# A two-layer graph kernel: the turn of the exponentials as a product with scaled diagonals, the mask put in by TensorE, the node products spread over the second pass

## The chip, the cores and the metric

The kernel runs on one core of a Trainium2 chip. The metric is the device time of one execution in microseconds (us). TensorE is called PE in the rows, VectorE DVE, ScalarE ACT, GpSimd POOL and SyncE SP.

## The reference

```python
h = relu(layernorm(x))                                  # x: 64 graphs x 128 nodes x 128 channels
# layer 0
D = abs(h[:, :, None, :] - h[:, None, :, :])            # every pair of nodes of a graph
s = leaky(batchnorm(D @ W1.T + b1), 0.01) @ W2.T + b2   # one score per pair; statistics over all pairs
A = softmax(where(adj > 0, s, -9e15), axis=-1)
y = leaky(batchnorm((A @ h) @ Wg.T + bg), 0.01)
x = x + concat([h, y]) @ Wt.T + bt
# layer 1: graph attention on relu(layernorm(x)) with W and a, softmax over the other axis, elu; x = x + that
```

All in float32, with 64 graphs.

## The kernel before

The 64 graphs are handled in couples of two and in 16 quads of four. Scores are symmetric, so a pair of nodes is computed once, by its distance d = 1 to 64. Eight distances of a couple make a chunk of 2 x 1024 columns: 8 chunks per couple, 16 per quad, 256 in all.

The first pass forms the products of W1 with the absolute differences of all chunks, for the statistics, and stores six of each eight chunks' products in DRAM (kept_products). The second pass goes over the chunks again, from the statistics on. A kept chunk is loaded by SP into a ring of ten buffers. The other two of each eight (numbers 2 and 7, "plain") are made again: VectorE subtracts (again, L294, both inputs in SBUF) and takes the absolute value (L1107), TensorE multiplies (L767). A plain chunk has one of two buffers, so again waits on prod2_ready until the products of the chunk before the last have read it. ScalarE applies batch norm and leaky ReLU to every chunk (L654), and TensorE multiplies by W2 (scores, L877) for each two chunks.

Around it each quad j has steps at fixed chunk numbers, written in one line: EVAC 24, DIST_T 25, TURN 27, SUM 41, SCORES 43, EXP 45, NORM 48, TURN_P 49, COPY 51, MIX 53, Y 56, Y_SUMS 57, each plus 16 j. Every engine runs the loop over n in its own queue and does its part of a step when it comes to it. In order:

- take_rows and turn_dist (L899) and take_turned (L1188) bring the scores to one row per node; POOL stores them askew to DRAM (L483), and loads them back (L489) so that row i holds its own distances; sum_half (L496) adds the part that wraps around. All this stands in POOL's one queue.
- att_sum (L906, L907) on TensorE forms s_half plus its transpose in att[0], a PSUM bank (4).
- att_scores on VectorE adds NEG times no_edge (L1204), takes the row maximum (L1207) and subtracts it (L1208). exps (L666) on ScalarE writes prob.
- att_norm on VectorE sums (L1213), takes the reciprocal (L1214) and multiplies prob with it (L1215).
- att_turn (L914) on TensorE transposes prob into att[1] (bank 5), att_copy (L1220) copies it to SBUF, att_mix (L921) multiplies it with h_nat, y_to_nodes (L662) and y_sums (L1224) finish.

h_nat holds at that time h times Wg: weighted_nodes (L852, eight passes for a quad) on TensorE and nodes_out (L632) on ScalarE make it. Quads 0 and 1 come before the second pass, and quads 2 to 15 in the first 21 chunks of it, two in each three chunks (mix_at), in banks 4 and 5 in turn. mask_l1 (L507) makes the mask of the second layer on POOL, in iterations 5 to 12. After the 256 chunks 59 more steps finish the last quads. Then comes the second layer.

Of the kernel before, what the change touches and what calls it, by code (L numbers as in the profile page):

```python
# [86 lines left out]
def two_layers(nc, x, adj, adj_t, w1_tt, wg_t, wt1_t, wt2_t, l1_w, l1_wt, cols, bt_rows,  # L87
# [8 lines left out]
    with ExitStack() as ctx:  # L96
# [51 lines left out]
        def late(at, n):  # L148
            return early[:, at:at + n]

        def by_graph(t):
# [6 lines left out]
        prob = by_graph(late(2048, 512))  # L158
# [17 lines left out]
        soft = sb("soft", [128, 4, 3, QUAD])  # L176

# [35 lines left out]
        s_sum, s_masked, dve_att, s_shifted, exp_done, prob_ready, prob_turned, prob_tr_ready, out_mm, y_ready = (  # L213
            sem(n) for n in ("s_sum", "s_masked", "dve_att", "s_shifted", "exp_done", "prob_ready", "prob_turned",
                             "prob_tr_ready", "out_mm", "y_ready"))
        x_out, x_folded = sem("x_out"), sem("x_folded")
# [81 lines left out]
        EVAC, DIST_T, TURN, SUM, SCORES, EXP, NORM, TURN_P, COPY, MIX, Y, Y_SUMS = 24, 25, 27, 41, 43, 45, 48, 49, 51, 53, 56, 57  # L298
# [58 lines left out]
        def _(sp):  # L357
# [35 lines left out]
            def load_half(j):  # L393
                sp.wait_ge(late_stored[j - BY_POOL], 16)
                sp.wait_ge(s_sum, j)
# [28 lines left out]
        def _(pool):  # L424
# [73 lines left out]

# [9 lines left out]

            for j in range(NQ):
                if j < BY_POOL:  # L510
                    store_skew(j)
                    load_half(j)
                sum_half(j)
                if 5 <= j < 5 + MRING:
                    mask_l1(j - 5)
            pool.wait_ge(bn2_var, 1)
# [8 lines left out]
        def _(act):  # L525
# [138 lines left out]
            def exps(j):  # L664
                act.wait_ge(s_shifted, j + 1)
                nc.scalar.activation(prob[:, :, :], s_shift[:, :, :], ACT.Exp).then_inc(exp_done, 1)  # L666

            for n in range(CHUNKS + TAIL):
# [10 lines left out]
                if mix_at(n) is not None:  # L679
                    nodes_out(mix_at(n))  # L680
# [53 lines left out]
        def _(pe):  # L734
# [146 lines left out]
            def at_zero(n):  # L881

                pe.wait_ge(weighted_ready, NQ)
# [4 lines left out]
            def at_one(n):  # L888

                pe.wait_ge(weighted_ready, NQ)  # L890
# [11 lines left out]
            def att_sum(j):  # L902
                pe.wait_ge(half_summed, j + 1)
                at_zero(QCH * j + SUM)
# [452 lines left out]
```

## Time and profile before

| | |
|---|---|
| median of 3 runs | 1147.15 us (1144.66 to 1148.58) |
| profiled execution | 1145.85 us, span of its instructions 1143.7 us |
| second pass | from 668 to about 1005 us, its last quads to 1037 us |
| busy, share of span | PE 92%, DVE 91%, ACT 88%, POOL 49% |
| mean granted TensorE clock | 0.987 of full |

The span is the time from the first to the last instruction. The remaining 2.15 us of the profiled execution lie around it. Busy shares are means over stages with different limits.

### The profile page before, as it was taken

The page shows a single profiled execution, that of the slowest core. Times are in us where ns is not written, and L with a number is a line of the kernel's source. Part 1 is how long each engine was busy: PE and PEld are TensorE (multiplying, and loading weights), DVE is VectorE, ACT ScalarE, POOL GpSimd, SP SyncE. Part 2 cuts the span into 40 slices and gives each one's busy share as a digit, 9 for nine tenths or more (in the row PEclk, how much of TensorE's full clock was granted, in tenths as well). Part 3 has the DMA queues.
Part 4 walks back from the last instruction along what each step waited for, and adds up shares of the span by engine and source line. Part 5 has one row for each costly group of instructions (what it writes and reads, how often), then busy time and mean ns, then how long its engine had stood idle before and what let it go on. Part 6 is the DMA issues. An engine that isn't in the chain of part 4 may idle for free.

```text
span 1143.7 us, 17677 instructions
## 1 busy us (share of the span) xinstructions
PE 1055.3 (92%) x6486; PEld 473.0 (41%) x6486; DVE 1037.4 (91%) x1382; ACT 1002.7 (88%) x1268; POOL 558.6 (49%) x314
## 2 busy tenths in 40 slices
PE   3999999999999999999999989999999999965997
PEld 1333333333333433333333444233333333355997
DVE  5999999999999999999999975999999999845887
ACT  4888999999999999999999969999999999814987
POOL 6586668777767867767777700111122213101420
PEclk9999999999999999999999989999999999987999
DMA  6443444444444444444444497999999999650012
GB/s 180 165 158 156 166 168 173 176 157 183 177 169 185 170 175 157 184 179 173 164 166 194 179 354 247 354 350 318 351 331 335 344 328 347 238 155 1 29 48 74
DMA packets 99059, 233.30 MB, mean 204 GB/s; under 512 B 9120, under 2 KB 46464, under 8 KB 98976
## 3 DMA queue, kind: packets, MB, share of 16 engines
q1 hardware_dynamic: 86704, 219.97, 52.4%
q0 software_dynamic: 2240, 7.34, 1.7%
q10 hardware_dynamic: 10032, 4.89, 1.6%
q8 instruction: 52, 0.85, 0.3%
q14 instruction: 31, 0.25, 0.1%
HBM read 124.43 MB, written 107.74 MB: 203 GB/s over the span
## 4 chain that ended last, share of the span: by engine, by line
PE 50%; DVE 27%; ACT 15%; issue 7%; ACTq 1%; POOL 0%; DMA 0%; DVEq 0%
PE psum L767 17%; DVE store L294 11%; PE psum L777 9%; ACT store L654 7%; PE psum L781 7%; DVE plain_st L1075 5%; PE psum L877 4%; ACT store L573 3%; PE psum L757 1%; PE psum L985 1%; DVE store L1107 1%; PE psum L967 1%; PE psum L950 1%; PE psum L968 1%; DVE ln_st L1012 1%
## 5 line engine op out<-in xcount | busy, mean ns | idle before, releaser
L294 POOL TENSOR_TENSOR store<-h_ext 128x2048 f32<-128x2048 f32 (+1 forms) x96 | 386.7, 4030 | 119.8 <-PE psum L767 115.9
L767 PE MATMUL psum<-store,w1tt_sb 128*64 128x512 f32 x1792 | 421.4, 598 | 19.4 <-ACT store L573 19.1
L294 DVE TENSOR_TENSOR store<-psum,h_ext 128x2048 f32<-128x2048 f32 x160 | 363.7, 2273 | 1.3 <-ACT h_ext L543 1.3
L573 ACT ACTIVATE store<-store 128x2048 f32<-128x2048 f32 x160 | 305.0, 1929 | 11.3 <-DVE store L294 8.1
L654 ACT ACTIVATE store<-store,st 128x1024 f32<-128x1024 f32 x192 | 227.9, 1240 | 0.0
L767 PEld LDWEIGHTS psum<-store,w1tt_sb 128*64 128x64 f32 x1792 | 122.2, 136 | 254.6 <-issue 224.8
L777 PE MATMUL psum<-store,w_twice 128*64 128x512 f32 x768 | 201.1, 601 | 7.0 <-DVE early L1040 3.5
L294 DVE TENSOR_TENSOR store<-h_ext 128x2048 f32<-128x2048 f32 x64 | 146.3, 2286 | 17.2 <-PE psum L767 17.2
L1075 DVE BATCH_NORM_STATS2 plain_st<-store 128x6 f32<-128x512 f32 x256 | 160.4, 676 | 0.0
L781 PE MATMUL psum<-early 128*64 128x512 bf16 x1152 | 158.2, 380 | 0.0
L877 PE MATMUL psum<-store,w_rows 128*32 128x512 f32 x1024 | 135.2, 610 | 8.9 <-ACT store L654 8.9
L585 ACT COPY store<-psum 128x1024 f32<-128x1024 f32 x128 | 128.6, 1022 | 4.7 <-PE psum L767 4.7
L781 PEld LDWEIGHTS psum<-early 128*64 128x64 bf16 x1152 | 69.3, 110 | 133.2 <-issue 114.8
L1075 DVE BATCH_NORM_STATS2 plain_st<-psum 128x6 f32<-128x512 f32 x128 | 82.3, 684 | 16.5 <-PE psum L767 16.4
L777 PEld LDWEIGHTS psum<-store,w_twice 128*64 128x64 f32 x768 | 53.1, 137 | 75.8 <-issue 30.9
L1107 DVE TENSOR_SCALAR store<-store 128x2048 int32<-128x2048 int32 x64 | 81.9, 1279 | 2.2
L654 ACT ACTIVATE store<-psum,st 128x1024 f32<-128x1024 f32 x64 | 76.7, 1198 | 5.6 <-issue 5.6
L496 POOL TENSOR_TENSOR early<-early 128x256 f32<-128x256 f32 x16 | 16.1, 1004 | 117.0 <-DMA early<-score_skew 117.0
L592 ACT ACTIVATE psum<-psum,st 128x1024 f32<-128x1024 f32 x64 | 69.8, 1091 | 1.6 <-DVE st L1138 1.6
L588 ACT ACTIVATE store<-psum 128x1024 f32<-128x1024 f32 x64 | 65.3, 1021 | 0.1
L483 POOL DMA_DIRECT2D score_skew<-early x14 | 11.4, 811 | 107.4 <-DVE early L1188 107.4
L463 POOL TENSOR_SCALAR no_edge<-early 128x256 uint8<-128x256 int32 x64 | 54.6, 853 | 0.0
(163 smaller groups left out, 1129.3 us busy)
## 6 DMA issues: line engine op xcount, KB each, us to landing
kept_products<-store SPq DMA_DIRECT2D x192, 512.0 KB, 2.7
store<-kept_products SPq DMA_DIRECT2D x192, 512.0 KB, 5.5
early<-score_skew POOLq DMA_DIRECT2D x14, 384.0 KB, 6.7
early<-adj SPq DMA_DIRECT2D x16, 256.0 KB, 3.6
early<-adj_t SPq DMA_DIRECT2D x16, 256.0 KB, 3.6
store<-x ACTq DMA_DIRECT2D x16, 256.0 KB, 5.3
out<-early SPq DMA_DIRECT2D x16, 256.0 KB, 2.3
score_skew<-early POOLq DMA_DIRECT2D x14, 128.0 KB, 6.0
```

The source lines that it names most:

```text
L294: return engine.tensor_tensor(t[:, :, 0:steps, :], nodes.unsqueeze(2).broadcast_to([C, 2, steps, N]), windows(h_ext[:, 2 * c, :], STEP * m ...
L573: nc.scalar.activation(t, t, ACT.Abs).then_inc(abs_ready, 1)
L585: nc.scalar.copy(kept[k % ZRING], tile).then_inc(kept_ready, 1)
L588: nc.scalar.activation(kept[k % ZRING], tile, ACT.Identity, accum_out=sum_p[:, t:t + 1])\
L592: nc.scalar.activation(tile, tile, ACT.Square, bias=sc(0), accum_out=sum_m[:, t:t + 1])\
L654: nc.scalar.activation(dst, src, ACT.Prelu, bias=sc(14), scale=sc(12), alpha=SLOPE0)\
L767: last = nc.tensor.matmul(t[MID * g:MID * g + MID, b, :], w1tt_sb[:, 0:MID], diff[slot][:, g, b * BANK:b * BANK + BANK], start=True, stop= ...
L777: nc.tensor.matmul(t[MID * g:MID * g + MID, b, :], w1_twice[:, :], diff[n % SLOTS][:, g, b * BANK:b * BANK + BANK], start=True, stop=False)
L781: last = nc.tensor.matmul(t[MID * g:MID * g + MID, b, :], y_parts[:, c % 4, s, MID * g:MID * g + MID], pair_nodes[:, k, b * BANK:b * BANK ...
L877: last = nc.tensor.matmul(score[j % 2][32 * q:32 * q + 32, :], w2_rows[:, r, :], src[:, b * BANK:b * BANK + BANK], start=(r == 0), stop=(r ...
L1075: last = nc.vector.bn_stats(plain_st[:, p, t, :], src[:, t, :])
L1107: nc.vector.tensor_scalar(bits, bits, 0x7FFFFFFF, None, ALU.bitwise_and).then_inc(diff2_ready, 1)
```

## The change

- The scores' bank att[0] now starts with one bfloat16 matmul of 512 columns, neg_ident (NEG on the diagonal) times none (no_edge as bfloat16, made by POOL in none_of, two buffers), then the transpose of s_half is added. VectorE adds s_half itself from SBUF in att_scores. s_half is so in use until s_masked, and the loads of the next one wait on that.
- exps works in place in s_shift. att_norm no longer multiplies: POOL's scale_ident scales four copies of the identity by the four columns of reciprocals, and att_turn is a float32 product of s_shift (stationary) with them. TURN_P goes from step 49 to 51. In POOL's queue scale_ident(j - 1) stands behind store_skew(j) and load_half(j), and ahead of sum_half(j); none_of(j) stands ahead of store_skew(j).
- Node products of quads 2 to 15 come one quad per 16 chunks, at n = 14 + 16 k, and their copies at 17 + 16 k, all but quad 1 in bank 4.

```diff
+        none = sb("none", [128, 2, BANK], BF16)
+        neg_ident = sb("neg_ident", [128, 128], BF16)
-        EVAC, ... NORM, TURN_P, COPY, MIX, Y, Y_SUMS = 24, 25, 27, 41, 43, 45, 48, 49, 51, 53, 56, 57
+        EVAC, ... NORM, TURN_P, COPY, MIX, Y, Y_SUMS = 24, 25, 27, 41, 43, 45, 48, 51, 51, 53, 56, 57
+        WEIGHED, WEIGHED_OUT = 14, 17
         def nodes_bank(u):
-            return psum[:, 4 + u % 2, :].rearrange("p (b n) -> p b n", b=QUAD)
-        def mix_at(n):
-            u, r = divmod(2 * n, 3)
-            return EARLY_MIX + u if r < 2 and 0 <= u < NQ - EARLY_MIX else None
+            return psum[:, 4 + (u == 1), :].rearrange("p (b n) -> p b n", b=QUAD)
+        def mix_at(n, step):
+            u, r = divmod(n - step, QCH)
+            return EARLY_MIX + u if r == 0 and 0 <= u < NQ - EARLY_MIX else None
...
             def load_half(j):
-                    pool.wait_ge(s_sum, j)
+                    pool.wait_ge(s_masked, j)
+            def none_of(j):
+                if j >= 2:
+                    pool.wait_ge(s_sum, j - 1)
+                nc.gpsimd.tensor_scalar(none[:, j % 2, :].rearrange("p (b n) -> p b n", b=QUAD), no_edge[0][:, quad(j), :],
+                                        1.0, None, ALU.mult).then_inc(none_set, 1)
+            def scale_ident(j):
+                pool.wait_ge(recip_ready, j + 1)
+                for b in range(QUAD):
+                    last = nc.gpsimd.tensor_scalar(scaled[:, b, :], ident[:, :], rows[:, 2, b:b + 1], None, ALU.mult)
+                last.then_inc(scaled_ready, 1)
             for j in range(NQ):
+                none_of(j)
                 if j < BY_POOL:
                     store_skew(j)
                     load_half(j)
+                if j > 0:
+                    scale_ident(j - 1)
                 sum_half(j)
...
-                nc.scalar.activation(prob[:, :, :], s_shift[:, :, :], ACT.Exp).then_inc(exp_done, 1)
+                nc.scalar.activation(s_shift[:, :, :], s_shift[:, :, :], ACT.Exp).then_inc(exp_done, 1)
...
             def weighted_nodes(u):
-                if u < 2:
+                if u < EARLY_MIX:
                     pe.wait_ge(kept_ready, NKEPT)
                 else:
-                    pe.wait_ge(weighted_ready, u - 1)
+                    at_zero(QCH * (u - EARLY_MIX) + WEIGHED)
...
-                for b in range(QUAD):
-                    nc.tensor.matmul(att[0][:, b, :], ident[:, :], s_half[:, b, 0:N], start=True, stop=False)
-                    last = nc.tensor.matmul(att[0][:, b, :], s_half[:, b, 0:N], ident[:, :], start=False, stop=True)
+                nc.tensor.matmul(att[0], neg_ident[:, :], none[:, j % 2, :], start=True, stop=False)
+                for b in range(QUAD):
+                    last = nc.tensor.matmul(att[0][:, b, :], s_half[:, b, 0:N], ident[:, :], start=False, stop=(b == QUAD - 1))
             def att_turn(j):
-                pe.wait_ge(prob_ready, j + 1)
+                pe.wait_ge(scaled_ready, j + 1)
                 at_one(QCH * j + TURN_P)
                 for b in range(QUAD):
-                    last = nc.tensor.transpose(att[1][:, b, :], prob[:, b, :], ident[:, :])
+                    last = nc.tensor.matmul(att[1][:, b, :], s_shift[:, b, :], scaled[:, b, :], start=True, stop=True)
...
             def att_scores(j):
                 if j > 0:
-                    dve.wait_ge(exp_done, j)
-                nc.vector.scalar_tensor_tensor(s_shift[:, :, :], no_edge[0][:, quad(j), :], NEG, att[0], ALU.mult, ALU.add)\
+                    dve.wait_ge(prob_turned, j)
+                nc.vector.tensor_tensor(s_shift[:, :, :], att[0], s_half[:, :, 0:N], ALU.add)\
                   .then_inc(s_masked, 1)
             def att_norm(j):
-                linked(nc.vector.tensor_reduce(rows[:, 1, :], prob[:, :, :], AX.X, ALU.add))
-                linked(nc.vector.reciprocal(rows[:, 2, :], rows[:, 1, :]))
-                nc.vector.tensor_tensor(prob[:, :, :], prob[:, :, :], bcast(rows[:, 2, :], N), ALU.mult)\
-                  .then_inc(prob_ready, 1)
+                linked(nc.vector.tensor_reduce(rows[:, 1, :], s_shift[:, :, :], AX.X, ALU.add))
+                nc.vector.reciprocal(rows[:, 2, :], rows[:, 1, :]).then_inc(recip_ready, 1)
```

## Rows read from the trace of the kernel before

**Rows 1.** The page, part 1: busy time, share of the span, instructions.
```profile
PE 1055.3 (92%) x6486; PEld 473.0 (41%) x6486; DVE 1037.4 (91%) x1382; ACT 1002.7 (88%) x1268; POOL 558.6 (49%) x314
```
**Rows 2.** Windows: length; busy PE, PEld, DVE, ACT, POOL; clock; DMA share; GB/s.
```profile
668.00:706.00 38.00, 37.18 (x234) 19.52 (x234) 23.83 (x18) 31.66 (x37) 0.00 (x0) 0.91 0.84 310
...
727.80:748.10 20.30, 19.80 (x136) 6.98 (x133) 19.59 (x21) 19.87 (x20) 2.62 (x4) 1.00 0.99 364
809.34:829.65 20.31, 19.40 (x132) 6.94 (x128) 20.02 (x22) 19.16 (x19) 4.70 (x4) 1.00 0.94 336
```
**Rows 3.** Timeline of ACT, 655 to 735 us: start, length, what.
```profile
668.21 1.23 ACT L654 ACTIVATE store<-store,st 128x1024 f32<-128x1024 f32 x1
671.18 0.59 ACT L632 COPY h_nat<-psum 128x512 f32<-128x512 f32 x1 [1.74 <-PE psum L852]
...
707.82 1.20 ACT L654 ACTIVATE store<-psum,st 128x1024 f32<-128x1024 f32 x1
...
726.86 2.40 ACT L654 ACTIVATE store<-store,st 128x1024 f32<-128x1024 f32 x2
```
**Rows 4.** Windows of L852 alone: length, PE busy, PEld busy, clock, DMA share, GB/s.
```profile
674.80:706.00 31.20, 13.37 (x96) 11.47 (x96) 1.00 0.80 287
```
**Rows 5.** Timeline of DVE over one quad from 809.34 us.
```profile
809.34 2.27 DVE L294 TENSOR_TENSOR store<-h_ext 128x2048 f32<-128x2048 f32 x1
...
812.79 0.61 DVE L1188 TENSOR_TENSOR early<-psum,last_mask 128x64 f32<-128x64 f32 x4
...
819.53 0.18 DVE L1214 RECIPROCAL rows<-rows 128x4 f32<-128x4 f32 x1
819.74 0.69 DVE L1215 TENSOR_TENSOR early<-early,rows 128x512 f32<-128x512 f32 x1
820.35 2.28 DVE L294 TENSOR_TENSOR store<-h_ext 128x2048 f32<-128x2048 f32 x1
822.67 1.23 DVE L1107 TENSOR_SCALAR store<-store 128x2048 int32<-128x2048 int32 x1
823.81 0.68 DVE L1220 COPY early<-psum 128x512 f32<-128x512 f32 x1
824.41 2.28 DVE L294 TENSOR_TENSOR store<-h_ext 128x2048 f32<-128x2048 f32 x1
```
**Rows 6.** Timeline of PE in the same quad.
```profile
810.05 0.39 PE L906 MATMUL psum<-early,ident 128*128 128x128 f32 x2
...
820.49 0.66 PE L914 MATMUL psum<-ident,early 128*128 128x128 f32 x4 [0.91 <-DVE early L1215]
...
822.07 1.94 PE L767 MATMUL psum<-store,w1tt_sb 128*64 128x512 f32 x8
...
824.93 1.16 PE L921 MATMUL psum<-early,h_nat 128*128 128x128 f32 x8
```
**Rows 7.** Timeline of POOL in the same quad.
```profile
820.05 0.75 POOL L489 DMA_DIRECT2D early<-score_skew  x1 [5.58 <-DMA score_skew<-early]
```
**Rows 8.** Lines by form on POOL, 0 to 70 us: busy us, mean ns.
```profile
L463 POOL TENSOR_SCALAR no_edge<-early 128x256 uint8<-128x256 int32 x5 | 4.3, 851 | 0.0
...
L292 POOL TENSOR_TENSOR store<-h_ext 128x128 f32<-128x128 f32 x2 | 0.9, 459 | 0.0
```
**Rows 9.** Timelines of POOL and of DVE near 845, 930 and 1023 us.
```profile
1022.80 0.73 POOL L496 TENSOR_TENSOR early<-early 128x256 f32<-128x256 f32 x1 [22.24 <-DMA early<-score_skew]
...
846.23 1.37 POOL L496 TENSOR_TENSOR early<-early 128x256 f32<-128x256 f32 x1 [6.08 <-DMA early<-score_skew]
...
844.73 2.28 DVE L294 TENSOR_TENSOR store<-h_ext 128x2048 f32<-128x2048 f32 x1
847.04 1.64 DVE L1107 TENSOR_SCALAR store<-store 128x2048 int32<-128x2048 int32 x1
...
930.22 1.49 POOL L507 TENSOR_SCALAR early<-no_edge 128x512 f32<-128x512 uint8 x1
...
931.24 2.27 DVE L294 TENSOR_TENSOR store<-h_ext 128x2048 f32<-128x2048 f32 x1
```

More of the change, by code:

```diff
@@ L157, in two_layers @@
         s_shift = by_graph(late(1536, 512))
-        prob = by_graph(late(2048, 512))
+        scaled = by_graph(late(2048, 512))
         prob_tr = by_graph(late(2560, 512))
@@ L212, in two_layers @@
         skew_cleared = [sem("skew_cleared0"), sem("skew_cleared1")]
-        s_sum, s_masked, dve_att, s_shifted, exp_done, prob_ready, prob_turned, prob_tr_ready, out_mm, y_ready = (
-            sem(n) for n in ("s_sum", "s_masked", "dve_att", "s_shifted", "exp_done", "prob_ready", "prob_turned",
+        s_sum, s_masked, dve_att, s_shifted, exp_done, recip_ready, prob_turned, prob_tr_ready, out_mm, y_ready = (
+            sem(n) for n in ("s_sum", "s_masked", "dve_att", "s_shifted", "exp_done", "recip_ready", "prob_turned",
                              "prob_tr_ready", "out_mm", "y_ready"))
+        none_set, neg_set, scaled_ready = sem("none_set"), sem("neg_set"), sem("scaled_ready")
         x_out, x_folded = sem("x_out"), sem("x_folded")
@@ L295, in subtract, with weighed_before @@
                                         windows(h_ext[:, 2 * c, :], STEP * m + 1, [2, steps, N], [EXT, 1, 1]), op)
[L298 removed]
+        EVAC, DIST_T, TURN, SUM, SCORES, EXP, NORM, TURN_P, COPY, MIX, Y, Y_SUMS = 24, 25, 27, 41, 43, 45, 48, 51, 51, 53, 56, 57
         TAIL = 59
         EARLY_MIX = 2
+        WEIGHED, WEIGHED_OUT = 14, 17
         def nodes_bank(u):
[L304 to L308 removed]
+            return psum[:, 4 + (u == 1), :].rearrange("p (b n) -> p b n", b=QUAD)
+        def mix_at(n, step):
+            u, r = divmod(n - step, QCH)
+            return EARLY_MIX + u if r == 0 and 0 <= u < NQ - EARLY_MIX else None
+        def weighed_before(n):
+            return min(EARLY_MIX + so_far(WEIGHED, n), NQ)
         BY_POOL = NQ - 2
@@ L394, in load_half @@
                 sp.wait_ge(late_stored[j - BY_POOL], 16)
-                sp.wait_ge(s_sum, j)
+                sp.wait_ge(s_masked, j)
                 sp.dma_start(s_half[:, :, :], skew_dram[j % 2].rearrange("b (i j) -> i b j", j=EXT))\
@@ L507, in mask_l1 @@
                 nc.gpsimd.tensor_scalar(MASK[j % MRING], no_edge[1][:, quad(j), :], NEG, None, ALU.mult).then_inc(mask_set, 1)
+            nc.gpsimd.tensor_scalar(neg_ident[:, :], ident[:, :], NEG, None, ALU.mult).then_inc(neg_set, 1)
             for j in range(NQ):
+                none_of(j)
                 if j < BY_POOL:
@@ L515, in _ @@
                     mask_l1(j - 5)
+            scale_ident(NQ - 1)
             pool.wait_ge(bn2_var, 1)
@@ L678, in _ @@
                         load_x(q)
-                if mix_at(n) is not None:
-                    nodes_out(mix_at(n))
+                if mix_at(n, WEIGHED_OUT) is not None:
+                    nodes_out(mix_at(n, WEIGHED_OUT))
                 for step, do in ((Y, y_to_nodes), (EXP, exps)):
@@ L881, in at_zero @@
             def at_zero(n):
-                pe.wait_ge(weighted_ready, NQ)
+                pe.wait_ge(weighted_ready, weighed_before(n))
                 for s, step in ((s_masked, SCORES), (y_out, Y)):
@@ L888, in at_one @@
             def at_one(n):
-                pe.wait_ge(weighted_ready, NQ)
+                pe.wait_ge(weighted_ready, EARLY_MIX)
                 for s, step in ((turn_ready, TURN), (prob_tr_ready, COPY)):
@@ L927, in _ @@
                     products_again(n + LEAD_PROD)
-                if mix_at(n) is not None:
-                    weighted_nodes(mix_at(n))
+                if mix_at(n, WEIGHED) is not None:
+                    weighted_nodes(mix_at(n, WEIGHED))
                 m = n - LAG_SCORE
```

3 lines of the change are left out of this document (added).

## The prediction

> **What bounds the kernel now.** I read the page first [rows 1]: three engines are busy for about nine tenths of the span, so no engine is the bound as a whole, and the stages have to be read one by one. The first pass and the last layer are not touched by the change (their code is the same), so only the stretch from 668 to 1037 us matters. I read it by windows [rows 2] and then by the timeline of each engine.
>
> *The opening, chunks 0 to 22.* ScalarE starts the first chunk's leaky ReLU at 668.21 and, 23 chunks on, chunk 23 at 707.82 [rows 3]. The next 17 chunks start 1.12 us apart ((726.86 - 707.82) / 17). TensorE is 37.2 of 38.0 us busy in the opening [rows 2], and 13.4 us of that in the 31 us from 674.8 are twelve of the fourteen quads of node products (L852) [rows 4]. So the opening is bound by TensorE, and by the node products in it.
>
> *The steady state, chunks 43 to 235.* One quad of 16 chunks takes 20.31 us; VectorE is busy for 20.0, TensorE 19.4, ScalarE 19.2 of it, and the DMA engines 94% [rows 2]. VectorE is the bound. Take one quad and call the start of L294 at 809.34 zero [rows 5]. The turn of the distances (L1188) starts at 3.45, the reciprocal (L1214) ends at 10.37, the scaling (L1215) follows, then L294 for chunk 58 at 11.01, its absolute value (L1107) at 13.33, the copy (L1220) at 14.47 and L294 for chunk 63 at 15.07. TensorE turns the probabilities at 11.15 and makes the products of chunk 55 at 12.73 to 14.67 [rows 6]. L294 for chunk 63 overwrites the buffer that those products read, so it must wait for them (the wait on prod2_ready): they end 0.4 us before it starts. That is the tightest place that the change touches.
>
> **What the change removes, adds and moves.**
>
> *Node products spread out.* The opening loses 12 to 14 quads of TensorE work and their copies on ScalarE. What is next there is ScalarE at 1.12 us a chunk: 23 chunks are 25.8 us instead of 39.6, less one copy that now comes at chunk 17 (L632, 0.59 long, 0.5 as a step between neighbours) [rows 3]: -13.3 us. VectorE's and TensorE's own work per chunk is below 1.12 there. The loads must keep up: six 0.52 MB tiles per 8 x 1.12 us are 350 GB/s, and 364 GB/s are shown with the DMA engines at 99% [rows 2], so the transfers just suffice. The copy at chunk 33 costs 0.5 again: **-12.8 us** until chunk 43. In the steady quads the node products add 8 passes, 1.1 us, to TensorE (as L921 [rows 6]) and 0.5 to ScalarE.
>
> *Mask by TensorE.* Sixteen passes of 0.11 us (L906, L907, 1.8 us) [rows 6] become eight passes and one bfloat16 matmul of 512 columns. TensorE gains about 0.65. L1204 stays one VectorE instruction of the same size from PSUM. The later release of s_half by s_masked instead of s_sum costs nothing: L1204 is done by about 4.7, and the load waits for its stored scores until 10.71 anyway [rows 5, 7].
>
> *Turn as product.* A transpose of four is 0.66 us, the product in float32 is eight passes like L921, 1.16 us: +0.5. TensorE's sum is 19.4 - 0.65 + 0.5 + 1.1 = 20.3 us a quad, ScalarE's 19.2 + 0.5 = 19.7; both are just hidden under 20.31, and would be the bound if VectorE gained.
>
> *Scaling moved.* VectorE loses L1215, 0.71 us a quad as the reciprocal's end, 10.37, and the next L294 show [rows 5]. POOL gets four tensor_scalar of 128x128 float32, each bounded by 0.2 (not under a quarter of L463's 256 columns) and 0.54 (two thirds of L463); between L292 of the same size, 0.46, and half of L463, 0.43, I take 0.43, 0.39 apart: 1.6 us [rows 8]. Ahead of them in POOL's queue stands the issue of the load (L489), which ends at 10.71 + 0.75 = 11.46 [rows 7], after the reciprocal.
>
> *The shared way into SBUF.* POOL and VectorE shut each other out [rows 9]. L496 of POOL, 0.73 us when alone (at 1022.80), starts at 846.23 while VectorE's L294 (both inputs in SBUF) runs, and takes 1.37: it gets through only when L294 ends at about 846.9. L1107, 1.23 us when alone, then stands at 847.04 and takes 1.64, as it waits for L496. So a POOL instruction issued during L294 is held to its end, and one still running holds L1107. But POOL's one-input L507 at 930.22 to 931.71 did not hold the L294 that started at 931.24 (2.27 us, its normal time). The Trainium skill (page "SBUF — State Buffer", section "Who interferes with whom") says that a VectorE instruction with two SBUF inputs contends with a POOL instruction that reads SBUF, and that the first one holds the ports for its whole length; L496 agrees with both, L507 at 930.22 not with the second.
>
> Now the new order, with L1215 gone: L294 for chunk 58 runs from 10.30 to 12.57, before POOL can start. The first of the four scalings waits for its end, 12.43, and runs to 12.86. L1107 is next in line and takes the way at 12.72 until 13.81. The other three follow: 13.81 + 2 x 0.39 + 0.43 = 15.02. TensorE then turns (15.08), starts the products of chunk 55 at 16.17 (1.09 later) and ends them at 18.11. L294 for chunk 63 starts at 18.14 instead of 15.07: **+3.07 us a quad**, for 13 quads (12 from chunk 43 to 235 and the next) **+39.9**. The bounds of one scaling move that by 3 x 0.2 down and 3 x 0.1 up a quad.
>
> *none_of on POOL.* One 128x512 instruction from uint8 a quad, like L507, 1.5 us. If it comes before L294 it is hidden; if it slips between L294 and L1107 it holds L1107 by up to 1.2. Bounds 0 and 1.2 per quad over 12 quads; the mask of the second layer (L507) adds to the crowd in seven of them. I take the middle, 0.6: **+7**.
>
> *The tail.* Quads 14 and 15 run as a bare chain. Each gains 0.65 in the sum and loses L1215 (0.7), but waits for four scalings (1.6 + 0.1) and for 0.5 more of turn: +0.8 each, **+1.6**.
>
> Sum: -12.8 + 39.9 + 7 + 1.6 = +35.7 us. On the profiled span that is 1143.7 + 35.7 = 1179.4, with the 2.15 us around it 1181.6 against 1145.85; on the median of the runs, which is 1.3 above the profiled one, 1182.9, say **1183 us**.
>
> **The rivals.**
>
> *A: as above,* 0.45.
>
> *B: the four scalings go through in one run* and L1107 waits for all four. Speaks for it: POOL's small instructions follow each other without a gap; against it: L1107 is in line first. The scalings end at 12.43 + 3 x 0.39 + 0.43 = 14.03, the products of chunk 55 at 17.12: +2.08 a quad, sum -12.8 + 27.0 + 7 + 1.6 = +22.8, 1170 us. 0.13.
>
> *C: L294 does not hold POOL's one-input instructions.* It is seen holding only a two-input one [rows 9]. Then they run from 11.46 to 13.06, products end at 16.15, +1.1 a quad or 14; with 5 for none_of -12.8 + 14.3 + 5 + 1.6 = +8, 1155 us. 0.20.
>
> *D: the other side, the scalings are out of the way in time.* Each quad comes out even if the last of the four ends by 15.07 - 3.12 = 11.95; that needs scalings near 0.2 us, POOL not held by L294 and an early L489. VectorE then gains its 0.7, but TensorE's 20.3 us takes over, so a quad stays at 20.3 and what is left is the opening: -12.8 + 1.6 = -11.2, 1136 us. The point where it decides is +1 us a quad: below that the kernel is faster. 0.17.
>
> *E: POOL's one-input instructions hold L294 as well,* for their whole length. none_of then costs its 1.2 wherever it falls before chunk 63's absolute value, +14 in place of +7, 1190 us. Against it speaks L507 at 930.22 [rows 9]: 0.05. This is what the rule of the Trainium skill's page "SBUF — State Buffer", section "Who interferes with whom", would do here.
>
> **How the numbers follow.** The prediction is A. The bounds of one scaling, times 13 quads, put A between 8 us less and 4 us more, those of none_of 7 us either way. The range 1142 to 1193 holds A, B, C and E with most of these bounds and leaves out D. A measurement of this kernel can tell about 0.3%, 3.4 us. Faster by more: D and the lowest end of C, 0.19. Within: the low part of C, 0.06. Slower: A, B, E and most of C, 0.75.
>
> **What would show it.** In the profile after: chunk 23 starts near 694 to 695 us on ScalarE if the opening is right. The scalings on POOL, at their first near the end of a VectorE L294 and with one of them stretched or spaced by about 1 us around L1107, tell A from B and C. VectorE's L1220 would show an idle time of 1.5 to 2 us for TensorE, and the L294 after it another of about 1 us released by L767. A quad would take 23 to 24.5 us and the DMA engines would fall from 94% to about 80%. The prediction is wrong if a quad stays near 20.3 us, or if the opening gains nothing because the loads can't keep 350 GB/s.

## The result

| | median us | runs |
|---|---|---|
| before | 1146.59 | 4 (1144.66 to 1148.58) |
| changed | 1212.43 | 4 (1211.25 to 1215.07) |

The changed kernel takes 1.0577 times as long, 95% interval 1.055 to 1.0605: 66 us more, where 36 were forecast. The profiled execution took 1211.25 us, span 1209.3. The direction was right, and the time lies above the range.

**The profile after.** Line numbers have moved: L294 is L298, L1107 L1137, L767 L794, L654 L681, L852 L879, L1188 L1218, L1214 L1244, L1220 L1248, L914 L944, L921 L951, L489 L498 and L1246 L1274. New are L518 (the scalings) and L511 (none_of). The page's first line, beside [rows 1]:

```profile
PE 1080.4 (89%) x6422; PEld 482.8 (40%) x6438; DVE 1028.2 (85%) x1366; ACT 1005.6 (83%) x1268; POOL 647.4 (54%) x395
```

Windows with the columns of [rows 2] (length; busy PE, PEld, DVE, ACT, POOL; clock; DMA share; GB/s): the opening, and two quads of the steady state (from one turn of the distances to the next).

```profile
668.90:706.90 38.00, 34.07 (x194) 9.44 (x198) 32.69 (x28) 35.55 (x33) 2.64 (x3) 0.87 1.01 387
...
848.72:874.26 25.54, 21.93 (x136) 8.65 (x133) 19.44 (x21) 19.92 (x21) 12.51 (x9) 0.93 0.79 270
874.26:899.91 25.65, 22.06 (x136) 7.90 (x133) 19.25 (x21) 19.89 (x20) 10.68 (x9) 0.93 0.75 265
```

A quad takes 25.5 us in the mean instead of 20.3. VectorE's work in it has fallen by 0.6 to 0.8 us and TensorE's busy time has risen by 2.6; the granted clock is 0.93 where it was 1.00, and the DMA engines fell from 94% to 77%. The timelines of one quad, its L298 for chunk 55 at 870.82 taken as zero like L294 at 809.34 in [rows 5, 6]:

```profile
870.82 2.27 DVE L298 TENSOR_TENSOR store<-h_ext 128x2048 f32<-128x2048 f32 x1
...
881.01 0.18 DVE L1244 RECIPROCAL rows<-rows 128x4 f32<-128x4 f32 x1
881.24 2.29 DVE L298 TENSOR_TENSOR store<-h_ext 128x2048 f32<-128x2048 f32 x1
883.56 1.28 DVE L1137 TENSOR_SCALAR store<-store 128x2048 int32<-128x2048 int32 x1
887.98 0.69 DVE L1248 COPY early<-psum 128x512 f32<-128x512 f32 x1 [3.14 <-PE psum L944]
891.27 2.29 DVE L298 TENSOR_TENSOR store<-h_ext 128x2048 f32<-128x2048 f32 x1 [2.60 <-PE psum L794]
...
881.30 5.44 POOL L518 TENSOR_SCALAR early<-ident,rows 128x128 f32<-128x128 f32 x4
...
886.79 1.16 PE L944 MATMUL psum<-early 128*128 128x128 f32 x8 [3.50 <-POOL early L518]
887.88 3.35 PE L794 MATMUL psum<-store,w1tt_sb 128*64 128x512 f32 x8
```

The order is the forecast one: reciprocal, L298 for chunk 58, L1137, then a wait for POOL through TensorE, the copy, and a second wait, for the products of chunk 55, ahead of L298 for chunk 63. Two things are longer. The four scalings end at 15.92 (forecast 15.02). Their row is a sum; the times of one (least, median, most, in ns) show what is in it:

```profile
L518 POOL TENSOR_SCALAR early<-ident,rows x64: 594/597/3688, 730.5 to 1094.2; 128x128 f32<-128x128 f32 x64
```

The longest, 3.69 us, is the first of the four at 881.30: it ends at 884.98, just behind L1137 (884.84). The other three then take 0.60 each. In all twelve quads it is the first alone that is long (1.7 to 3.7 us), and it ends when L1137 has ended. And the products of chunk 55 take 3.35 us, not 1.94, so L298 for chunk 63 starts at 20.45 (forecast 18.14). Windows of the same stretch, columns as in [rows 2], show why the products were slow:

```profile
876.80:883.20 6.40, 6.36 (x46) 1.95 (x40) 6.28 (x6) 6.25 (x7) 2.66 (x2) 1.00 0.93 313
883.20:886.80 3.60, 0.10 (x5) 0.01 (x1) 1.61 (x2) 3.60 (x4) 3.60 (x5) 1.00 0.99 369
886.80:888.00 1.20, 1.20 (x10) 1.08 (x12) 0.02 (x1) 1.20 (x2) 1.11 (x2) 1.00 0.99 399
888.00:890.40 2.40, 2.40 (x8) 0.55 (x8) 0.68 (x1) 0.18 (x1) 2.31 (x2) 0.55 0.51 200
```

TensorE works 0.10 us of 3.60 while it waits for POOL. The turn right behind still runs at 1.00. Then the granted clock falls to 0.55, near its lower level of 1.2 GHz, for 2.4 us; it is 0.76 over the next 2.6 us and 1.00 from 893 to 899. The Trainium skill (page "TensorE: Matmul & The Clock Gate", section "Part 1: The HAM clock gate (the "warmup" mystery)") says that TensorE's clock is halved when it idles and released by activity; the trace agrees. The waits from 735 to 1035 us (total, times, longest) show both steps:

```profile
DVE early L1248 <- PE psum L944: 43.1, 12, 4.1
PE psum L944 <- POOL early L518: 42.5, 12, 3.6
DVE store L298 <- PE psum L794: 26.4, 17, 2.6
```

**Where the 65.6 us of span are.** Measured between the starts of the turn of the distances (TURN):

| stretch | before | after | difference | forecast |
|---|---|---|---|---|
| to chunk 43 | 731.50 | 722.22 | -9.3 | -12.8 |
| 12 quads, 43 to 235 | 243.85 | 305.59 | +61.7 | +43.8 |
| 235 to 251 | 17.79 | 24.38 | +6.6 | +3.1 |
| 251 to 267 | 21.52 | 21.45 | -0.1 | |
| 267 to the statistics (L1246, L1274) | 22.18 | 27.66 | +5.5 | +1.6 |
| second layer | | | +1.1 | 0 |

### The profile page after: what moved, and what is told of

Its sections match the earlier page's. It is cut to its first block, busy times and chain, and to the rows that moved or that the text cites. A ratio compares the mean times of both kernels' runs of the same rounds, so it can differ in the third digit from the quotient of the medians.

```text
span 1209.3 us, 17642 instructions
## 1 busy us (share of the span) xinstructions
PE 1080.4 (89%) x6422; PEld 482.8 (40%) x6438; DVE 1028.2 (85%) x1366; ACT 1005.6 (83%) x1268; POOL 647.4 (54%) x395
## 4 chain that ended last, share of the span: by engine, by line
PE 50%; DVE 21%; ACT 8%; POOL 7%; issue 7%; DMA 6%; ACTq 0%; DVEq 0%
PE psum L794 19%; DVE store L298 10%; PE psum L804 9%; PE psum L808 6%; DMA score_skew<-early 6%; POOL early L518 6%; DVE plain_st L1105 5%; PE psum L904 3%; ACT store L600 3%; PE psum L944 2%; ACT store L681 2%; PE psum L951 1%; PE psum L784 1%; PE psum L1015 1%; PE psum L997 1%
## 5 line engine op out<-in xcount | busy, mean ns | idle before, releaser
L794 PE MATMUL psum<-store,w1tt_sb 128*64 128x512 f32 x1792 | 435.0, 615 | 20.3 <-ACT store L600 19.1
L298 POOL TENSOR_TENSOR store<-h_ext 128x2048 f32<-128x2048 f32 (+1 forms) x96 | 386.7, 4030 | 119.9 <-PE psum L794 115.9
L298 DVE TENSOR_TENSOR store<-psum,h_ext 128x2048 f32<-128x2048 f32 x160 | 363.8, 2274 | 1.4 <-ACT h_ext L570 1.4
L794 PEld LDWEIGHTS psum<-store,w1tt_sb 128*64 128x64 f32 x1792 | 124.9, 140 | 254.9 <-issue 227.1
L681 ACT ACTIVATE store<-store,st 128x1024 f32<-128x1024 f32 x192 | 226.5, 1234 | 0.0
L298 DVE TENSOR_TENSOR store<-h_ext 128x2048 f32<-128x2048 f32 x64 | 146.8, 2294 | 37.5 <-PE psum L794 35.7
L904 PE MATMUL psum<-store,w_rows 128*32 128x512 f32 x1024 | 138.8, 619 | 10.1 <-ACT store L681 10.0
L612 ACT COPY store<-psum 128x1024 f32<-128x1024 f32 x128 | 128.6, 1023 | 4.7 <-PE psum L794 4.7
L681 ACT ACTIVATE store<-psum,st 128x1024 f32<-128x1024 f32 x64 | 76.9, 1202 | 60.4 <-PE psum L794 55.6
L518 POOL TENSOR_SCALAR early<-ident,rows 128x128 f32<-128x128 f32 x64 | 68.9, 1089 | 43.2 <-DVE rows L1244 42.7
L1137 DVE TENSOR_SCALAR store<-store 128x2048 int32<-128x2048 int32 x64 | 79.7, 1246 | 2.2
L944 PE MATMUL psum<-early 128*128 128x128 f32 x128 | 25.7, 363 | 53.0 <-POOL early L518 53.0
L1248 DVE COPY early<-psum 128x512 f32<-128x512 f32 x16 | 11.1, 691 | 67.7 <-PE psum L944 67.7
```

Source lines behind the costliest of these rows:

```text
L298: return engine.tensor_tensor(t[:, :, 0:steps, :], nodes.unsqueeze(2).broadcast_to([C, 2, steps, N]), windows(h_ext[:, 2 * c, :], STEP * m ...
L518: last = nc.gpsimd.tensor_scalar(scaled[:, b, :], ident[:, :], rows[:, 2, b:b + 1], None, ALU.mult)
L612: nc.scalar.copy(kept[k % ZRING], tile).then_inc(kept_ready, 1)
L681: nc.scalar.activation(dst, src, ACT.Prelu, bias=sc(14), scale=sc(12), alpha=SLOPE0)\
L794: last = nc.tensor.matmul(t[MID * g:MID * g + MID, b, :], w1tt_sb[:, 0:MID], diff[slot][:, g, b * BANK:b * BANK + BANK], start=True, stop= ...
L904: last = nc.tensor.matmul(score[j % 2][32 * q:32 * q + 32, :], w2_rows[:, r, :], src[:, b * BANK:b * BANK + BANK], start=(r == 0), stop=(r ...
```

## The experiments

**Undoing the turn alone.** The mask by TensorE and the spread node products stay; the exponentials are multiplied on VectorE and transposed as before, and TURN_P is 49.

```diff
-                nc.scalar.activation(s_shift[:, :, :], s_shift[:, :, :], ACT.Exp).then_inc(exp_done, 1)
+                nc.scalar.activation(scaled[:, :, :], s_shift[:, :, :], ACT.Exp).then_inc(exp_done, 1)
...
-                    scale_ident(j - 1)
...
-                nc.vector.reciprocal(rows[:, 2, :], rows[:, 1, :]).then_inc(recip_ready, 1)
+                linked(nc.vector.reciprocal(rows[:, 2, :], rows[:, 1, :]))
+                nc.vector.tensor_tensor(scaled[:, :, :], scaled[:, :, :], bcast(rows[:, 2, :], N), ALU.mult)\
+                  .then_inc(scaled_ready, 1)
...
-                    last = nc.tensor.matmul(att[1][:, b, :], s_shift[:, b, :], scaled[:, b, :], start=True, stop=True)
+                    last = nc.tensor.transpose(att[1][:, b, :], scaled[:, b, :], ident[:, :])
```

> The changed kernel with only its turn undone: exponentials scaled by VectorE and transposed at step 49 as before; the mask by TensorE with none_of on POOL and the spread node products stay. Theory 1 (the chain from the reciprocal over POOL's four scalings, held at the way into SBUF, to the turn, the products of chunk 55 and the L298 after them makes the loss): a quad returns to 20.3 us, the opening keeps its 9 us, the tail gains 0.65 for each of two sums: span 1143.7 - 9.3 - 1.3, about 1133, and about 1136 us for the run, 1% faster than before. Theory 2 (the loss comes from the fuller TensorE queue and from none_of crowding the way into SBUF): a quad stays above 22 us and the run above 1160.

Measured: 1139.97 us (4 runs), ratio 0.9941, interval 0.9919 to 0.9963; quads of 20.8 to 21.1, not 20.3. So the new turn costs 72 us (1212.43 - 1139.97) and the rest of the change gains 6 to 7, less than its opening gives: the quads were expected at 20.3.

**The scaling on VectorE, all else as changed.**

```diff
-                if j > 0:
-                    scale_ident(j - 1)
...
-                nc.vector.reciprocal(rows[:, 2, :], rows[:, 1, :]).then_inc(recip_ready, 1)
+                linked(nc.vector.reciprocal(rows[:, 2, :], rows[:, 1, :]))
+                for b in range(QUAD):
+                    last = nc.vector.tensor_scalar(scaled[:, b, :], ident[:, :], rows[:, 2, b:b + 1], None, ALU.mult)
```

> The changed kernel with the four scaled diagonals made by VectorE (four tensor_scalar of 128x128 right after the reciprocal) instead of POOL; turn as a product, mask and nodes stay. Theory 1: VectorE pays about 1.0 for them in place of the 0.7 of before, the turn is done by 12.6 us of the quad, nothing waits: a quad of 20.6 to 20.9, about 1140 to 1145 us. Theory 2: TensorE with 20.3 us of work and none_of still crowd: over 1160.

Measured: 1142.88 us in one execution, quads of 20.8, later 21.1. The four scalings take 0.9 us there. The product as such, with its in-place exponentials, costs about 3 us over the whole kernel (one execution against a median of four, and the turn at 51 instead of 49); what costs the other 70 is that POOL makes the diagonals.

**The turn behind the products.** TURN_P 52, COPY 53, MIX 55 put the turn of the exponentials after the products of chunk 55 in TensorE's queue.

```diff
-        ..., NORM, TURN_P, COPY, MIX, Y, Y_SUMS = ..., 48, 51, 51, 53, 56, 57
+        ..., NORM, TURN_P, COPY, MIX, Y, Y_SUMS = ..., 48, 52, 53, 55, 56, 57
```

> The changed kernel with TURN_P, COPY and MIX at 52, 53 and 55 instead of 51, 51 and 53, so that TensorE makes the products of chunk 55 before it waits for the scalings. Theory 1: the scalings still end about 15.9 us into the quad, the copy at 17.8, and L298 for chunk 63 starts there instead of at 20.4: a quad of 22.8 to 23.2 instead of 25.5, 1176 to 1184 us. If the wait of those products were not on the path, nothing would change (1212).

Measured: 1167.77 us in one execution, faster than expected, with quads of 22.3 to 23.0. Timelines of VectorE, POOL and TensorE:

```profile
870.98 0.69 DVE L1248 COPY early<-psum 128x512 f32<-128x512 f32 x1 [3.14 <-PE psum L944]
871.59 2.28 DVE L298 TENSOR_TENSOR store<-h_ext 128x2048 f32<-128x2048 f32 x1
...
864.46 5.27 POOL L518 TENSOR_SCALAR early<-ident,rows 128x128 f32<-128x128 f32 x4 [0.61 <-DVE rows L1244]
...
869.78 1.16 PE L944 MATMUL psum<-early 128*128 128x128 f32 x8 [0.47 <-POOL early L518]
```

The scalings are about as slow as in the changed kernel and the copy waits the same 3.14 us, but L298 follows the copy at once, and TensorE idles only 0.47 us: the clock is 1.00 over the steady quads. Both the second wait and the clock's part are gone, 45 us.

**TensorE kept busy.** Fourteen bfloat16 matmuls into att[1] stand ahead of the wait for the diagonals (at_one, the turn's other wait, moves ahead of them too); the turn then overwrites what they wrote.

```diff
+                for _ in range(14):
+                    nc.tensor.matmul(att[1], neg_ident[:, :],
+                                     neg_ident[:, :].unsqueeze(1).broadcast_to([128, QUAD, C]), start=True, stop=True)
                 pe.wait_ge(scaled_ready, j + 1)
```

> The changed kernel with 14 bfloat16 matmuls of 512 columns (3.0 us, into the bank that the turn then overwrites) ahead of TensorE's wait for the scalings. Theory 1 with the clock as a part of it: the granted clock stays at 1.00 where it was 0.93, and the turn and the products behind the wait take 1.2 and 1.9 us instead of up to 2.1 and 3.4; a quad falls by 0.9 to 1.4 us, the run to 1194 to 1200. If the clock is not on the path: 1212, no change.

Measured: 1192.75 us in one execution, quads of 24.07. TensorE's timeline:

```profile
875.80 3.19 PE L943 MATMUL psum<-neg_ident 128*128 128x512 bf16 x14
879.42 1.16 PE L946 MATMUL psum<-early 128*128 128x128 f32 x8 [0.43 <-POOL early L518]
880.51 1.94 PE L794 MATMUL psum<-store,w1tt_sb 128*64 128x512 f32 x8
```

The turn waits for the same scalings, but the products take 1.94 us again, and a quad loses 1.4 of its 5.15 us. The clock is 18 to 20 us of the whole loss (18.5 of the span, 19.7 of the time; one execution).

**One POOL instruction instead of four**, with two inputs in SBUF, 128x512:

```diff
-                for b in range(QUAD):
-                    last = nc.gpsimd.tensor_scalar(scaled[:, b, :], ident[:, :], rows[:, 2, b:b + 1], None, ALU.mult)
+                nc.gpsimd.tensor_tensor(scaled[:, :, :], ident[:, :].unsqueeze(1).broadcast_to([N, QUAD, N]),
+                                        bcast(rows[:, 2, :], N), ALU.mult)
```

> The changed kernel with the four scalings as one POOL tensor_tensor of 128x512 (identity and reciprocals both broadcast). Theory 1, as refined by the trace after: a one-input POOL instruction reads in the gap between L298 and L1137 but can't write until L1137 has ended, so all four end 2 us after it; a two-input one, like L496 before, goes through whole in that gap and holds L1137. It takes about 0.2 + 512 x 2.06 ns = 1.25 us, ends 13.8 us into the quad instead of 15.9, the products of chunk 55 end at 16.9 at full clock, a quad takes 22.0 to 22.4, the run 1168 to 1174 us. If two inputs make no difference at the way into SBUF, it ends at 15.1, a quad takes 24 to 24.7, the run 1190 to 1202.

Measured: 1157.10 us in one execution, quads of 21.1 to 22.2, better than expected. POOL and VectorE:

```profile
860.61 3.15 POOL L517 TENSOR_TENSOR early<-ident,rows 128x512 f32<-128x512 f32 x1 [0.16 <-DVE rows L1243]
...
860.57 2.29 DVE L298 TENSOR_TENSOR store<-h_ext 128x2048 f32<-128x2048 f32 x1
862.90 1.95 DVE L1136 TENSOR_SCALAR store<-store 128x2048 int32<-128x2048 int32 x1
865.01 0.69 DVE L1247 COPY early<-psum 128x512 f32<-128x512 f32 x1 [0.17 <-PE psum L943]
```

It waits for L298 and is done at 863.76, 0.9 us behind it, while VectorE's absolute value is held for it (1.95). In the changed kernel the four small ones were done 3.2 us behind L298 and held L1137 by only 0.05. So the large one passes between two of VectorE's, where the first of the four small ones is not through before the second has ended as well. The large one is also less work: with nothing of VectorE beside it, it takes 1.04 us (at 1009.52), where the four take 2.35. How much of the 55 us comes from that and how much from the passing was not tried apart.

**VectorE waits for the scalings** before L298 for chunk 58, so that they meet nothing:

```diff
+                    if quad_at(n, COPY) is not None:
+                        dve.wait_ge(scaled_ready, quad_at(n, COPY) + 1)
```

> The changed kernel, but VectorE waits for scaled_ready before the L298 of chunk 58, so that none of its instructions stands beside the scalings. Theory 1: the scalings take 2.35 us in one piece and end 13.9 us into the quad; VectorE loses 3.5 us of work there and still L298 for chunk 63 starts at 18.0 instead of 20.4: a quad of 23.0 to 23.4, 1180 to 1186 us, so VectorE idle is better than VectorE busy. If the way into SBUF were not what stretches the scalings, they would stay at 5 us and the quad grow to 28, the run to 1240.

Measured: 1166.59 us in one execution, faster than expected, with quads of 22.0 to 23.5. POOL and VectorE:

```profile
865.05 2.35 POOL L518 TENSOR_SCALAR early<-ident,rows 128x128 f32<-128x128 f32 x4 [0.61 <-DVE rows L1244]
...
867.43 2.29 DVE L298 TENSOR_TENSOR store<-h_ext 128x2048 f32<-128x2048 f32 x1 [2.49 <-POOL early L518]
```

Unhindered, the four take 2.35 us, 0.59 each; under VectorE's two instructions they take 5.27 and 5.44 in the two quads shown above, all of the difference in the first of them. Standing still for 2.49 us is 46 us better than running alongside, since neither of the later waits, for the turn and for the products of chunk 55, is left.

**The node products alone**, spread as in the change, in the kernel before. The diff, beside the waits on weighted_ready that go with it:

```diff
-            return psum[:, 4 + u % 2, :].rearrange("p (b n) -> p b n", b=QUAD)
+            return psum[:, 4 + (u == 1), :].rearrange("p (b n) -> p b n", b=QUAD)
...
-            u, r = divmod(2 * n, 3)
-            return EARLY_MIX + u if r < 2 and 0 <= u < NQ - EARLY_MIX else None
+            u, r = divmod(n - step, QCH)
+            return EARLY_MIX + u if r == 0 and 0 <= u < NQ - EARLY_MIX else None
```

> The kernel before with the node products alone spread (mask and turn as before). Theory 1: the opening gains its 9 us; TensorE has 19.4 + 1.1 = 20.5 us a quad, so a quad takes 20.3 to 20.7, and the run 1138 to 1143. Set against the run with mask and nodes (20.8 to 21.1 a quad, 1140.0 us) it shows what none_of on POOL costs: if that is the 0.5 by which those quads are longer than before, quads here are 20.3 to 20.4 and the run about 1137; if it is TensorE's load, they are 20.8 here as well.

Measured: 1140.92 us (7 runs), ratio 0.9946, interval 0.9929 to 0.9963; quads of 20.82, all alike. VectorE and ScalarE:

```profile
862.43 0.69 DVE L1228 BATCH_NORM_STATS2 bst<-h_nat 128x6 f32<-128x512 f32 x1 [0.51 <-ACT h_nat L666]
...
853.39 0.57 ACT L636 COPY h_nat<-psum 128x512 f32<-128x512 f32 x1
...
861.71 0.69 ACT L666 ACTIVATE h_nat<-psum,col 128x512 f32<-128x512 f32 x1
```

VectorE's sums of y wait 0.51 us for ScalarE, whose queue now has the copy of the node products in it. That is the 0.5 us that the spread costs a quad, as the wait reads; the next two runs try it. Beside the run without the turn it also shows that mask and none_of together cost or gain nothing measurable (1140.92 against 1139.97).

**The sums of y later**, place 59 instead of 57, in the version without the new turn and in the one with the node products alone:

```diff
-        ..., TURN_P, COPY, MIX, Y, Y_SUMS = ..., 49, 51, 53, 56, 57
+        ..., TURN_P, COPY, MIX, Y, Y_SUMS = ..., 49, 51, 53, 56, 59
```

> The version with bfloat16 mask and spread node products, and the turn as before (1139.97 us, quads 20.8 to 21.1), with the sums of y taken two places later in the quad (place 59 instead of 57), behind the VectorE row that now waits for ScalarE. If the 0.5 us per quad that the spread node products cost comes from ScalarE's copy of their result, which delays the operands of those sums, the wait is covered and the quads are 20.3 to 20.45 again: about 1134 us. If it comes from TensorE's load or from POOL's mask instruction, nothing changes: 1140 us.

> The kernel before with the node products spread and the sums of y two places later. By the theory of ScalarE's copy: quads of 20.3 to 20.45 where spreading alone gave 20.82, about 1135 us. By the rival (TensorE's load) 1141 us, as without the later sums.

Measured: 1137.63 us (6 runs), ratio 0.9924, interval 0.991 to 0.9939, the fastest kernel of the study and 0.8% under the kernel before, though its interval overlaps that of the version with the sums at 57; and 1139.62 us (4 runs), ratio 0.9947, interval 0.9929 to 0.9966, not told apart from 1140.92. Both fell short of what was expected (1134 and 1135). The first has quads of 20.28 up to 802 us, as expected, and of 20.6 to 21.0 after it. From there on the mask of the second layer (L529) stands ahead of none_of (L511) in POOL's queue, and POOL's instructions meet VectorE's:

```profile
876.14 2.75 DVE L298 TENSOR_TENSOR store<-h_ext 128x2048 f32<-128x2048 f32 x1
...
881.02 2.71 DVE L298 TENSOR_TENSOR store<-h_ext 128x2048 f32<-128x2048 f32 x1
...
904.05 1.51 DVE L1134 TENSOR_SCALAR store<-store 128x2048 int32<-128x2048 int32 x1
...
876.01 0.74 POOL L505 TENSOR_TENSOR early<-early 128x256 f32<-128x256 f32 x1 [4.65 <-DMA early<-score_skew]
...
880.99 1.49 POOL L511 TENSOR_SCALAR none<-no_edge 128x512 bf16<-128x512 uint8 x1
...
902.50 3.52 POOL L511 TENSOR_SCALAR none<-no_edge 128x512 bf16<-128x512 uint8 x1
```

L511 now ends behind L1134, which takes 1.51 us instead of 1.23; that is the 0.3 us of most of these quads. That row is of the quad behind the other two rows. In their quad, one of the longest, L298 is held twice as well. Once it is by L505, which has two inputs and started 0.13 us earlier (2.75 instead of 2.28), and once beside L511, which has one input and started 0.03 us earlier (2.71).

The second has quads of 20.57: with the wait for ScalarE gone, the same kernel waits for TensorE's products, by half as much:

```profile
860.46 2.29 DVE L294 TENSOR_TENSOR store<-h_ext 128x2048 f32<-128x2048 f32 x1 [0.28 <-PE psum L771]
```

So both theories had a part: ScalarE's copy makes the wait of 0.5, and with it gone TensorE's load still costs 0.25 a quad (20.57 against 20.32), which the bfloat16 mask takes away (20.28).

**The node products early, in the changed kernel.** Beside this, nodes_bank and the waits on weighted_ready are as in the kernel before.

```diff
-            u, r = divmod(n - step, QCH)
-            return EARLY_MIX + u if r == 0 and 0 <= u < NQ - EARLY_MIX else None
+            u, r = divmod(2 * n, 3)
+            return EARLY_MIX + u if r < 2 and 0 <= u < NQ - EARLY_MIX else None
```

> The changed kernel with the node products all in the opening, as in the kernel before. The quads are set by the chain of POOL's scalings, the products and the copies, which node products don't touch: periods of 25.0 to 25.5 as in the changed kernel, the opening longer by the 9 us that the spreading gave, about 1220 us. If the node products took part in the loss inside the quads, these are 0.5 to 1 us shorter and the time is 1209 to 1214 us.

Measured: 1227.69 us in one execution; 1220 was expected. The opening loses 10.5 us, and the quads are not equal but longer, 26.2 us in the mean, 9 us in twelve; 3.3 us come back behind chunk 235. TensorE, and a window of it:

```profile
929.30 2.07 PE L944 MATMUL psum<-early 128*128 128x128 f32 x8 [3.33 <-POOL early L518]
931.30 3.68 PE L794 MATMUL psum<-store,w1tt_sb 128*64 128x512 f32 x8
```

```profile
929.20:931.30 2.10, 2.00 (x8) 1.78 (x8) 0.00 (x0) 1.18 (x2) 0.66 (x2) 0.50 1.01 394
```

Here the turn already runs at 0.50, the lower level. The mean clock from 748 to 998 us is 0.89, against 0.94 in the changed kernel. Without the 1.2 us of node products per quad TensorE is at the lower clock for longer: work that was thought neutral had held part of the clock, as these rows read.

**All causes taken away together.** One POOL instruction, the turn late, and the sums of y at 59:

> The changed kernel with three edits together: one POOL instruction with two inputs for the four scaled diagonals, the turn and what follows it one or two places later (TURN_P, COPY, MIX 52, 53, 55), and the sums of y at place 59. If the loss is made only of the wait for the scaled diagonals ahead of the products, VectorE's wait behind them and the late sums, nothing of it is left: VectorE saves 0.69 us of multiplication and gives back 0.7 by the held absolute value, TensorE works 20.3 to 20.8 us a quad, so the quads are 20.4 to 20.8, and the time 1135 to 1142 us, as without the new turn (1137.63 us). If a loss by the product as such or by POOL's share of the memory ports remains, quads of 21.5 or more and 1150 us or above.

Measured: 1161.46 us (5 runs), ratio 1.0133, interval 1.0117 to 1.015; quads of 21.8 to 22.5. A miss, and slower than the one instruction alone (1157.10). VectorE:

```profile
865.15 0.69 DVE L1247 COPY early<-psum 128x512 f32<-128x512 f32 x1 [1.93 <-PE psum L943]
```

The diagonals are ready in time, but the turn now stands behind the products of chunk 55, while the copy still stands ahead of L298 for chunk 63 in VectorE's queue. In the last run the copy stands behind it:

```diff
-        ..., TURN_P, COPY, MIX, Y, Y_SUMS = ..., 52, 53, 55, 56, 59
+        ..., TURN_P, COPY, MIX, Y, Y_SUMS = ..., 52, 56, 56, 56, 60
```

> The three edits of the run before (1161.46 us, quads 22.1) and the copy of the turned probabilities behind the second subtraction too (COPY, MIX, Y, Y_SUMS 56, 56, 56, 60). In the run before, the copy still stood ahead of that subtraction in VectorE's queue and waited 1.93 us for TensorE's turn. If that wait was all that was left, nothing of the chain through POOL holds VectorE any more: the quads are bound by TensorE's own work, 20.4 to 20.8 us, and the time is 1134 to 1142 us. If there is a loss by the product itself or by POOL's share of the ports, the quads stay at 21.5 us or more and the time above 1150 us.

Measured: 1153.09 us (10 runs), ratio 1.0051, interval 1.0035 to 1.0066; quads of 21.4. A miss again: the wait is gone, 8 us, but not all of the loss. VectorE, POOL, TensorE and ScalarE:

```profile
858.22 2.69 DVE L298 TENSOR_TENSOR store<-h_ext 128x2048 f32<-128x2048 f32 x1 [0.58 <-PE psum L793]
...
857.72 1.04 POOL L517 TENSOR_TENSOR early<-ident,rows 128x512 f32<-128x512 f32 x1 [0.60 <-DVE rows L1243]
...
859.72 1.06 PE L903 MATMUL psum<-store,w_rows 128*32 128x512 f32 x8 [0.55 <-ACT store L680]
...
869.72 0.69 ACT L688 ACTIVATE h_nat<-psum,col 128x512 f32<-128x512 f32 x1 [1.82 <-PE psum L950]
```

The wait has moved on: ScalarE's queue stands 1.8 us for the products with h_nat, which now come late; its activations, TensorE's scores and products behind them are late, and VectorE waits 0.58 and 0.53 us in this quad. POOL has a part too: L517 starts 0.5 us ahead of L298, which takes 2.69 us instead of 2.28, and L1136 at 870.16 takes 1.51 instead of 1.23 beside none_of. Two waits of 1.1, 0.4 and 0.3 by POOL, less the 0.7 of the multiplication, are the last 1.1 us a quad. This sum was read from the rows of one quad and not tried.

## Why the prediction was right in sign and wrong in size

**The step that failed is the size of the stall in "The shared way into SBUF":** +3.07 us a quad where the trace has 5.38 for the start of L298 for chunk 63 (20.45 against 15.07). That step had the two waits right, but not where the first scaling goes and how long one takes, and it had no term for the clock. The difference splits into two parts:

- *The scalings, +0.90.* They were forecast to end at 15.02: the first through between L294 and L1107, by 12.86, the other three behind L1107 from 13.81 on, 0.43 long and 0.39 apart. The first did not get through there. It ends at 14.16, behind L1137, so that the other three start 0.35 later. And one takes 0.60, above the upper bound of 0.54 that I had from L463 (two thirds of 0.851 are in fact 0.57, and 0.60 is above that too): three take 1.76 instead of 1.21, another 0.55.
- *The clock, +1.41.* The forecast put it at nothing, without a reason. It let TensorE wait for a turn at 15.08 and had the products behind it run at their usual 1.94. They take 3.35. The filled run gives back 1.4 us a quad, and shows the part by itself.

3.07 + 0.90 + 1.41 is 5.38, and this quad is 5.3 longer (25.63 against 20.31). The mean of the twelve is 5.15, as one of them, from 747.68 on, took only 24.08. The 0.6 a quad for none_of, +7 in all, was a wrong term as well: L511 at 889.09 runs while VectorE waits and costs nothing, and in only two of the twelve quads did one hold L1137, by 0.28 (1.51 at 868.12). So the forecast of 43.8 for 12 quads had 36.8 for the stall and 7 for none_of, and the 61.7 hold next to nothing for none_of.

- *Opening:* -9.3, forecast -12.8. Chunk 23 was to start near 694.5 and starts at 698.01; the second pass itself begins 1.0 us later than before (669.23 against 668.21). ScalarE's timeline shows most of the rest:

```profile
678.30 1.20 ACT L681 ACTIVATE store<-psum,st 128x1024 f32<-128x1024 f32 x1 [1.09 <-PE psum L794]
...
682.91 1.21 ACT L681 ACTIVATE store<-psum,st 128x1024 f32<-128x1024 f32 x1 [1.15 <-PE psum L794]
...
698.01 1.20 ACT L681 ACTIVATE store<-psum,st 128x1024 f32<-128x1024 f32 x1
```

Two waits for products, 2.2 us, where I had said that TensorE's work per chunk is below 1.12. That holds at full clock only. A row of TensorE, and the window from 674 us after and before:

```profile
674.57 3.68 PE L794 MATMUL psum<-store,w1tt_sb 128*64 128x512 f32 x8 [0.90 <-DVE store L1137]
...
674.00:680.00 6.00, 5.43 (x20) 1.27 (x24) 5.64 (x4) 4.91 (x5) 0.00 (x0) 0.50 1.04 386
...
674.00:680.00 6.00, 6.00 (x42) 2.81 (x35) 4.74 (x3) 4.48 (x6) 0.00 (x0) 0.94 1.05 382
```

The products that ScalarE waits for at 678.30 take 3.68 us instead of 1.94, at the lower clock. By an estimate from these rows, at 1.94 they would end at 676.5, before ScalarE is free at 677.2, and the first wait would be gone; the second comes from what stands behind them in TensorE's queue. From 668 to 674 us TensorE was busy for 2.52 us, and for 5.25 in the kernel before, where node products filled it. The run with mask and nodes, the one with the nodes alone and the filled one had a clock of 0.64, 0.61 and 0.63 in this window. So the clock is what the forecast left out here too; that the missing node products let it stay low is read from these rows. The loads kept up (387 GB/s).

- *Node products in the quads:* 1.1 us on TensorE and 0.5 on ScalarE were costed at nothing, since both stay under 20.31. The sums held, but ScalarE's 0.5 lies ahead of a row that VectorE needs: 0.5 a quad when VectorE is the bound (the run with node products alone), 6 us. In the changed kernel it is hidden, and with the node products moved back the quads were longer (26.2 against 25.5).
- *Tail:* +5.5, forecast +1.6. The last quad shows both mis-sized terms bare:

```profile
1094.88 2.08 PE L944 MATMUL psum<-early 128*128 128x128 f32 x8 [5.16 <-POOL early L518]
...
1092.48 2.35 POOL L518 TENSOR_SCALAR early<-ident,rows 128x128 f32<-128x128 f32 x4 [10.16 <-DVE rows L1244]
```

The scalings take 2.35 instead of 1.6, and the turn as product 2.08 at a granted clock of 0.50, where the transpose takes 0.66 in the same place.

- *The rivals.* B and C are out: the four scalings neither passed ahead of L1137 nor ran through L298. D too, as the kernel is slower. E is out as well: none_of cost nearly nothing. By the rule of the Trainium skill (page "SBUF — State Buffer", section "Who interferes with whom") the instruction that comes first holds the ports for its whole length. For POOL's two-input instructions the trace agrees: L517 waits for the end of L298 and L1136 (1.95) for the end of L517, in twelve of thirteen quads; in the other one, L517 started at 796.02, 0.08 us behind L298, and ran its 1.04 us at once while L298 took 3.29. For the one-input ones it does not: the first scaling is still held when L298 has ended and L1137 begins, and L511, which started ahead of L298 at 881.02, held it by 0.43 us of its own 1.49.

Nothing explains the 1.1 us of the second layer; it was not tried.

## What to carry to other kernels

A step handed from the fullest engine to an idle one is paid by its way back: here 0.7 us of VectorE was given for four scalings on POOL that end 5.4 us after they start, held by VectorE's own instructions, with TensorE waiting in between and everything in its queue behind. When a forecast makes TensorE idle for some microseconds in each round of a loop, price the work right behind at the lower clock too; the same goes for the start of a stage from which TensorE's work is taken away. And look at both queues when a late result is moved: it helps only if the consumer's place moves behind the other work as well, and then the next consumer's queue has to be read in the same way.

## What the hardware showed that I had not expected

- Four 128x128 float32 scalings on POOL with a scalar per partition take 2.35 us undisturbed; VectorE makes them in 0.9. Beside VectorE's subtraction and absolute value they take up to 5.44, and only the first is longer (3.69): it ends just behind the absolute value, and the other three run at 0.60. They cost the absolute value 0.05 us.
- One 128x512 instruction of POOL with two inputs does the same work in 1.04 us undisturbed. Issued during the subtraction it passes ahead of the absolute value and costs it 0.72. Whether the number of inputs or the size makes this difference was not tried, and why the small one is held so long is not shown.
- An idle stretch of 3.5 us in TensorE was followed by 1.2 us of work at a clock of 1.00 and then by 2.4 us at 0.55; one of 0.47 us left it at 1.00.
